# Three changes to the order of TensorE's work between the state sums of a scan: a gate half, a row product, and four gate projections

## The reference, cut to what matters

```python
# conditioning part
ctx  = causal_ema(x, tau_ctx)
gate = sigmoid(cat(x, ctx) @ Wg.T + bg)             # 256 channels: two halves of 128
mod  = sigmoid(gelu(x @ Wn1.T + bn1) @ Wn2.T + bn2) # 8 rows
...                                                 # 8 gated causal traces, mixed, then layernorm -> y
# mixer
xc, z = split(y @ W_in.T)
xc    = silu(conv4(xc) + conv_b)
dt, B, C = split(xc @ W_x.T)                        # 64, 16 and 16 rows
delta = softplus(dt @ W_dt.T + b_dt)
for n in range(16):                                 # 16 states, each a scan over 512 tokens
    h_n = scan(exp(delta * A[n]) * h + delta * B[n] * xc)
    out += C[n] * h_n
out = (out + D * xc) * silu(z)
x = x + out @ W_out.T
```

## Time and profile before

| | |
|---|---|
| median of 3 runs | 4055.92 us (4038.67 to 4058.45) |
| profiled execution, its time | 4052.32 us |
| its span, first to last instruction | 4050.5 us |
| DVE busy over the span | 2396.0 us (59%) |
| PE busy over the span | 3383.1 us (84%) |
| ACT busy over the span | 1485.8 us (37%) |

### The profile page before, as it was taken

The page is one execution under the profiler, slowest core; times in us unless marked ns, Lnnn a source line. Parts: engine busy times, 40 slices in busy tenths (PEclk is TensorE's granted clock), DMA queues, the critical chain, the costliest instruction groups (busy, mean ns, idle before and its releaser), DMA issues. The chain is left out here.

```text
span 4050.5 us, 36523 instructions
## 1 busy us (share of the span) xinstructions
PE 3383.1 (84%) x10476; PEld 1695.8 (42%) x10477; DVE 2396.0 (59%) x2992; ACT 1485.8 (37%) x2754; POOL 632.3 (16%) x753
## 2 busy tenths in 40 slices
PE   4788888787878786589969999999999999978991
PEld 2233333333323332256624444444444444436771
DVE  4599999999999999622214343434343344342335
ACT  2545444453535353133313232332323232323440
POOL 0000202020202020123300011010101010106771
PEclk9899999999989898799979999999999999988995
DMA  2122222222222222422120101010101010135447
GB/s 78 48 73 82 78 85 72 86 74 80 76 79 76 82 74 81 162 83 66 61 107 1 33 19 41 10 50 6 46 5 46 5 46 5 46 137 165 151 148 272
DMA packets 160948, 297.58 MB, mean 73 GB/s; under 512 B 27618, under 2 KB 84578, under 8 KB 159586
## 3 DMA queue, kind: packets, MB, share of 16 engines
q1 hardware_dynamic: 136914, 236.09, 18.1%
q0 software_dynamic: 20352, 57.17, 3.9%
q10 hardware_dynamic: 3600, 3.35, 0.2%
HBM read 202.37 MB, written 94.16 MB: 73 GB/s over the span
## 5 line engine op out<-in xcount | busy, mean ns | idle before, releaser
L1147 PE MATMUL ps<-hs,ident 128*128 128x512 f32 x1024 | 544.6, 682 | 238.8 <-DVE hs L1256 238.8
L1250 DVE TENSOR_TENSOR_SCAN hs<-dA,hs 128x2048 f32<-128x2048 f32 x128 | 565.4, 4417 | 6.7
L409 POOL COPY rows<-new_slot 128x64 f32<-128x64 f32 x48 | 25.6, 562 | 2920.2 <-DVE new_pl L535 2897.2
L1834 PE MATMUL ps<-pT,V 128*128 128x512 f32 x1024 | 449.3, 593 | 7.0 <-DVE pT L1942 7.0
L1205 ACT ACTIVATE dA<-dl,w_An 128x511 f32<-128x511 f32 x512 | 326.0, 709 | 339.1 <-DVE hs L1250 337.4
L1147 PEld LDWEIGHTS ps<-hs,ident 128*128 128x128 f32 x1024 | 217.6, 219 | 553.3 <-DVE hs L1256 284.0
L1242 DVE TENSOR_TENSOR hs<-u,bb 128x2048 f32<-128x2048 f32 x128 | 292.4, 2284 | 10.1 <-PE ps L1147 9.4
L1256 DVE TENSOR_TENSOR hs<-hs,cb 128x2048 f32<-128x2048 f32 x128 | 289.9, 2266 | 0.0
L1834 PEld LDWEIGHTS ps<-pT,V 128*128 128x128 f32 x1024 | 190.2, 190 | 226.8 <-issue 218.1
L1379 POOL DMA_INDIRECT slots<-og,idt x232 | 241.8, 1042 | 272.7 <-DVE og L1467 197.7
L405 POOL DMA_INDIRECT sorted<-rows,new_pl x192 | 266.3, 1387 | 63.6 <-issue 43.9
(11 more groups left out here) (292 smaller groups left out, 5116.3 us busy)
## 6 DMA issues: line engine op xcount, KB each, us to landing
bb<-bcd SPq DMA_DIRECT2D x128, 256.0 KB, 3.5
cb<-bcd SPq DMA_DIRECT2D x128, 256.0 KB, 3.2
xg<-sorted SPq DMA_DIRECT2D x232, 136.0 KB, 2.1
slots<-zeros SPq DMA_DIRECT2D x136, 128.0 KB, 3.2
mb<-modd SPq DMA_DIRECT2D x64, 256.0 KB, 4.0
qrg<-slots SPq DMA_DIRECT2D x16, 1024.0 KB, 8.4
rg<-slots SPq DMA_DIRECT2D x36, 256.0 KB, 3.3
w_Lr<-in_Lora SPq DMA_DIRECT2D x9, 576.0 KB, 3.7
```

The source lines that it names most:

```text
L1147: ins = pe.matmul(ps[:, j, :], ident[:, :], m.hs[:, N % 3, j, :], start=False, stop=(N % NS == NS - 1))
L1250: dve.tensor_tensor_scan(state, m.dA[:, N % 2].rearrange("p j t -> p (j t)"), state, 0.0, ALU.mult, ALU.add).then_inc(s_h, 1)
L1834: ins = pe.matmul(ps[:, 6 + j, :], V[:, m, h * D + j * P:h * D + (j + 1) * P], pT[:, i % 2, h % 2, m, :], start=(h == 0 and m == 0), stop= ...
```

## The change

Three products change their place in PE's order. Nothing is added or removed, and DVE, ACT, GpSimd and SyncE keep their instructions in the same order. (a) Gate half 1 moves from step 2, behind `add_state` of state 1, to the end of step 1, in front of it. (b) The B and C row product moves from the end of step 11, in front of `add_state` of state 11, to the start of step 12, behind it. (c) `gate_products` moves from the end of step 13 to the end of step 15.

```diff
+        def gate_half(pe, c, j):
+            product(pe, ps[:, 7, :],
+                    [(Wg[:, i, j * P:(j + 1) * P], x[:, i, :]) for i in range(DC)]
+                    + [(Wg[:, DC + i, j * P:(j + 1) * P], c.cx[:, i, :]) for i in range(DC)], c_gate)
...
-            if n in (1, 2):
-                j = n - 1
-                if j == 0:
-                    pe.wait_ge(c_ctx, DC * (k + 1))
-                    if k:
-                        pe.wait_ge(m_sz, JI * k)
-                else:
-                    pe.wait_ge(c_wg, DC * k + 1)
-                product(pe, ps[:, 7, :],
-                        [(Wg[:, i, j * P:(j + 1) * P], x[:, i, :]) for i in range(DC)]
-                        + [(Wg[:, DC + i, j * P:(j + 1) * P], c.cx[:, i, :]) for i in range(DC)], c_gate)
             if n == 1:
+                pe.wait_ge(c_ctx, DC * (k + 1))
+                gate_half(pe, c, 0)
                 pe.wait_ge(c_hg, k + 1)
                 product(pe, ps[0:NTR, 6, :], [(Wn2[:, :], h1[:, :])], c_md)
+                pe.wait_ge(c_wg, DC * k + 1)
+                gate_half(pe, c, 1)
...
             elif n == 11:
                 pe.wait_ge(m_xs, JI * (k + 1))
                 product(pe, ps[0:DTR, 4, :], [(Wxd[:, i, :], m.xs[:, i, :]) for i in range(JI)], m_dt)
+            elif n == 12:
                 product(pe, ps[0:2 * NS, 5, :], [(Wxbc[:, i, :], m.xs[:, i, :]) for i in range(JI)], m_bc)
-            elif n == 12:
                 pe.wait_ge(m_dts, k + 1)
...
-                                if n == 13:
+                                if n == 15:
                                     gate_products(kc)
```

## The result

The changed kernel takes 4084.59 us (median of 5 runs, 4083.95 to 4088.88) against 4055.92 for the one before: a ratio of 1.0088, 95% interval 1.0062 to 1.0113. By the medians it is slower by 29 us, or 0.7%; the ratio is larger because the runs of the kernel before lie in two groups, here two of five at 4039 to 4040 us and three at 4056 to 4058. 4088 was forecast.

The account below looks back on a forecast made before the run. DVE was taken to bound the block loop. Terms of 1.55 + 1.65 + 2.1 - 0.5 = 4.8 us over seven blocks gave 33.6 us on 4052.32, 4086, stated as 4088 us for the median; range 4062 to 4104.

Parts of the forecast that it names:

- (a): Step 3: `into` waits for the later add of state 1, so DVE's gating comes later; +1.55 us a block.
- (b): Step 14: ACT's copy, decays, softplus and Ln come later, so DVE's L929 does too; +1.65 us a block.
- (c): Block end: add 14 starts slow after longer idle time, `gate` waits for add 15; +2.1 us a block (1.3 to 2.85).
- Sum: Block loop: 1.55 + 1.65 + 2.1 - 0.5 = 4.8 us for each of seven blocks, 33.6 us in all.
- Bound: Block loop: DVE bounds it, busy 1454.87 of 1506.60 us; reordering PE could give back at most 27 us.
- The credit for `skip_term`: Block boundary: PE's denser run keeps `skip_term` at full clock in about every third block; -0.5 us a block.
- C: Block loop: removed DVE waits are not replaced, `into` of state 4 finds its add done; 4035 us, chance 0.04.
- D: Block loop: gains and losses cancel, within 20 us of the time before, about 4060 us; chance 0.12.
- B: Block loop: `skip_term` and adds around it at full clock in every block; +21 us, 4075 us, chance 0.15.

Follow-up runs that it names:

- The fourth slot: Only move (a) on the kernel before, plus a fourth state-buffer slot, with three of four chunks' convolution weights left out: 4035.72 us (one run, only block loop compared).
- `skip_term` by banks: The kernel before, with `skip_term` waiting for `gate` bank by bank instead of for all four: 4036.32 us against 4055.39, ratio 0.9957.
- the copy behind the decays: Only move (b) on the kernel before, with ACT's copy of the B and C rows written behind step 12's four decays: 4047.52 us, ratio 0.9979.
- The filler: Only move (c) on the kernel before, plus ten unread matmuls in a free bank ahead of add 14: 4050.97 us (one run).
- part (a) alone: The kernel before with only gate half 1 moved ahead of `add_state` of state 1: 4065.43 us against 4055.23, ratio 1.0024.
- The fillers: The filler above, and `skip_term` by banks plus three unread matmuls ahead of the wait for y in step 8: 4032.65 us, ratio 0.9953.
- part (b) alone: The kernel before with only the B and C row product moved behind `add_state` of state 11: 4050.21 us against 4055.23, ratio 0.9989.

## Why the prediction was right, point by point

**Sum.** Over the loop 33.6 us were forecast and 31.1 came: 7.4 against 5.9 for (a) with its credit, 11.6 against 8.8 for (b), 14.7 against 15.0 for (c), nothing against 1.4 for the last block. The sum gives 4085.9 us from the profiled execution, or 4089.5 with the 3.6 us that the prediction adds for the median; the 4088 that it states is neither, and the changed kernel's median lay only 0.6 above its profiled execution. The upper end of its range is 4108 by its own terms (4098 and half of 20), not 4104; nothing hangs on it.

**Bound.** DVE is the bound in the loop, and the time changed by DVE's idle time alone: busy time within 2 us, idle time up by 30.

**(a), +1.55 us a block.** Right. 32.36 against 30.81 and 33.8 to 33.9 against 32.4, 36.9 against 35.3 in block 0, and the wait of 2.33 to 3.50 us lies in the 1.7 to 3.5 foreseen. The fourth slot shows its path. `skip_term` by banks shows that the price is not fixed: with PE 1.8 us earlier it is 0.6.

**(b), +1.65 us a block.** Right in place and path, 0.15 us too high: 1.50 us at either clock (alone 55.92 against 54.42, 57.62 against 56.09). The scan waited 0.67 to 2.37 us, L927 0.84 us where about 1 was foreseen. In the changed kernel the stretch grew by 8.8 us and not 7 x 1.65 = 11.6, because its products with y were slow in four blocks against five. The path over ACT's order is shown by the copy behind the decays.

**(c), +2.1 us a block.** The sum over the loop was right, 15.0 against 14.7, partly by luck. At the first six boundaries it cost 1.2 to 2.2 us, 11.0 in all, 1.8 on average. At the last one it cost 4.0 (from 23.84 to 27.82 us): there no next sequence exists, so the 2.33 us in which DVE scans x for it, which lie ahead of `gate` at the other boundaries and cover part of add 15's delay, are missing. I had taken that boundary as equal to the others. The 6.0 us taken for the late add measured 5.89 in the block shown and 5.2 to 6.3 over the boundaries. The filler shows that this slow start is what makes the loss against the kernel before; the place alone costs 0.8 us, less than the 1.1 that the slow add 15 had cost.

**The credit for `skip_term`, -0.5 us a block.** Here the reason was wrong and the size came near by luck. `skip_term` ran at full clock in four of the six blocks in which its lateness counts, and before in one of six. Against 6 x 1.55 = 9.3 us the stretch grew by 4.3, a credit of 5.0 us in all where 3.5 were forecast. But the denser run of part (c) did not earn it: part (a) alone, without that run, also has four of six, and the filler, with a denser run still, one of six. What decides it was not found.

The Trainium skill (TensorE: Matmul & The Clock Gate, section "Why this matters for your kernels") advises keeping TensorE continuously busy and leaving no idle gaps between bursts. The fillers agree: with unread matmuls in the gap add 14 takes 3.70 us, where it took 5.2 to 6.6 without them, and the products with y 7.13 in place of 8.83. The prediction let this rule count against part (c) by the longer gap, and that is in the runs; it also let it count for part (c) by the denser run ahead of `skip_term`, and that is not, as said above.

The rivals: C fell by the wait of `into` in every block. D is what part (b) alone did, and not the change. B's condition, `skip_term` at full clock, held in four blocks and not in all, without the reason that B gave for it, and add 14 was at its best (5.22 us) at one boundary of seven.

One term had no place in the sum: 1.4 us in the last block, where nothing was moved. The traces show where most of it comes from. The last two adds stand behind 3.51 us of idle time, and `gate` waits for them. In the kernel before and in the changed one they read:

```profile
1669.70 8.83 PE L1147 MATMUL ps<-hs,ident 128*128 128x512 f32 x16 [3.51 <-DVE hs L1256]
1698.56 9.88 PE L1145 MATMUL ps<-hs,ident 128*128 128x512 f32 x16 [3.51 <-DVE hs L1254]
```

The mean granted clock over them was 0.81 and 0.72, and `gate` waited 6.72 and 7.77 us, 1.05 us more. In all 13 kernels they took 7.1 to 10.0 us, and the wait of `gate` was 2.1 us less than that each time (7.13 us at a clock of 1.00 and a wait of 5.03 with (b) alone).

## What to carry to other kernels

Before moving a product past an instruction that another engine waits for, look at both queues: what stood right behind it on its own engine, and what stands behind its consumer on the consumer's engine. A wait that vanishes in front of the bounding engine is worth little if the next item in either queue has less slack than the move takes from it: here the moves took 3.4 to 3.6 us, and the slack was 0.07 us for `into` and 1.65 us on ACT. Where a wait repeats with the same length in some blocks and is missing in others, as the 1.58 us here, look for a matmul group at half clock upstream before reordering anything; shortening the idle time in front of `skip_term` by waiting bank by bank gave 0.4%, while three reorderings lost 0.7 to 0.9%. And before crediting a change with a faster clock, try the parts that should not change the clock: two of them did here.

## What was not expected of the hardware

The clock after the same idle time differs from block to block. Behind 2.54 to 2.58 us of idle time `skip_term` took 3.70 us in some blocks and 5.1 to 5.4 in others, and the products with y 7.13 or 8.83 us. Part (b) alone, which touches neither `skip_term` nor the gating, turned it from slow to fast at five boundaries and from fast to slow at one. Behind 0.78 us of idle time it took 3.70 us every time. So an edit in one place is paid or paid back in another, and the parts do not add: alone +10, -5 and +4 us, together +29. Why a given block falls on one side was not tested.
